# State space stage: both channel halves of a state in one VectorE product and scan and one GpSimd product of 1024 columns

## Chip, core and metric

The program runs on one core of a Trainium2 chip: TensorE (matmul), VectorE (DVE), ScalarE (ACT), GpSimd (POOL), and SyncE (SP), which issues the transfers. The metric is the time of one execution on the device in microseconds, here the median of three runs.

## What is computed

The reference is a network of two layers on 16 sequences of 256 positions with 128 features. Only the mamba block inside it is touched. It is, with 256 channels and 16 states a channel:

```python
h = layernorm(x, ln_g, ln_b)
xs, gate = jnp.split(h @ in_w, 2, axis=-1)
xs = jax.nn.silu(depthwise_conv(xs, conv_w) + conv_b)        # 4 taps
Bm, Cm = jnp.split(xs @ xp_w, 2, axis=-1)
dt = jax.nn.softplus(Bm @ dt_w + dt_b)
A = -jnp.exp(A_log)

def step(hst, inp):
    xt, dtt, Bt, Ct = inp
    dA = jnp.exp(dtt[..., None] * A)
    hst = hst * dA + dtt[..., None] * Bt[:, None, :] * xt[..., None]
    return hst, jnp.sum(hst * Ct[:, None, :], -1)
...
y = (y + D_skip * xs) * jax.nn.silu(gate)
return y @ out_w + res
```

## The kernel before

`state_space` (L1811) is one of fourteen stages that run one after the other. It goes through 8 turns (`TURNS`) of two sequences each. A tile has the 128 channels of one half (`CT` = 2 halves) on its partitions and the 512 positions of the two sequences (`T2`) as columns. For each of the 16 states (`N`) and each half, that is for 32 slots `w_` in a turn (`WS`), five engines pass one tile on:

- ScalarE, `decay` (L2074): dA = exp(A dt), 510 columns, into one of four places of dA. The first column of each sequence stays zero, which restarts the scan.
- TensorE, `spread_b` (L2223), once a state: the row of B spread over 128 partitions, into one of two PSUM banks BB, two states ahead.
- VectorE, `inflow` (L2122): the product of du = dt x and B, into one of two PSUM banks BU. It is issued one slot ahead, so the product of slot u+1 stands in front of the scan of slot u.
- VectorE, `scan` (L2132): the recurrence along the columns, into one of four places of hs.
- GpSimd, `weigh` (L1984): hs times the row of C, into one of four places of hc. SyncE fetches that row for all partitions, four states ahead (`Cs`).
- TensorE, `add_up` (L2230): hc through the identity, summed over the 16 states in the PSUM banks YS. It runs two slots behind.

Each of these waits for the engine that reads its place to be done with it. With four places, the scan of slot u waits for the product of slot u-4 on GpSimd, `weigh` for the sum of slot u-4, and `decay` for the scan of slot u-4.

All other work of a turn is written into the same loops by slot, in the tables `DVE_AT`, `POOL_AT`, `ACT_AT` and `PE_AT`. Most of it prepares the next turn: `stats` and `apply` (layer norm, VectorE; four `tensor_scalar` at L2119), `power` (GpSimd), `hn` and `h` (ScalarE), the transposes `h`, the convolution `x0` and `x1` (slots 10 and 11), `g0` and `g1`, `bc`, `dt0` and `dt1` (TensorE), `silu`, `bc`, `abs`, `exp`, `log` (ScalarE), and on GpSimd `split` (B in three bfloat16 parts), `dt` and `du`. The PSUM banks F0 and F1 are handed round among TensorE's pieces in the order of their issue. The rest, `gate`, `out` and `add`, finishes the turn before. An engine takes its queue in order, so a piece that waits holds every later slot on that engine. TensorE's queue at slot 10, for example, is `spread_b` of state 7, `add_up` of slot 8, `x0`.

## Time and profile before

| | |
|---|---|
| median of 3 runs | 4903.26 us (4899.63 to 4903.86) |
| profiled execution | 4894.49 us, its span 4892.8 us |
| VectorE busy over the span | 3405.3 us (70%) |
| TensorE / GpSimd / ScalarE busy | 3823.4 / 2392.6 / 2341.8 us |
| state space stage, first product to last sum | 545 us, 11% of the span |
| VectorE's product and scan in it | 256 of 695 ns and 256 of 1212 ns |
| GpSimd's product | 256 of 1271 ns |

The shares over the whole span are means over fourteen stages with different limits. For this change the stage has to be read alone: first the table of windows for it, then its groups of instructions, then the timeline of one of its turns.

### The profile page before, as it was taken

Reading aid. Unit: us, or ns where it says so; the run is one execution under the profiler, and the core shown is the slowest. Engines: PE = TensorE matmul, PEld = TensorE weight load, DVE = VectorE, ACT = ScalarE, POOL = GpSimd, SP = SyncE. Lnnn points to the kernel's source line nnn. Section 1 sums busy time; section 2 is a strip of 40 time slices with the busy share of each in tenths; the row PEclk is TensorE's granted clock in tenths of the full one; section 3 lists DMA queues with packets and bytes.
Section 4 is the critical chain, followed back from the end, with each engine's and each line's share of the span. In section 5 each row is a group of like instructions: output and inputs, shape, how many; then the busy total and the mean of one; then the engine's idle time right before and its main releaser. Section 6 shows DMA issues by size and latency. Waiting matters only on the chain. (4 is left out here: it accounts for less than half of the span.)

```text
span 4892.8 us, 90894 instructions
## 1 busy us (share of the span) xinstructions
PE 3823.4 (78%) x25840; PEld 2727.7 (56%) x25840; DVE 3405.3 (70%) x9524; ACT 2341.8 (48%) x5537; POOL 2392.6 (49%) x3948
## 2 busy tenths in 40 slices
PE   7889797779999799468868947568776887699475
PEld 5666565656666466366656636523332665466365
DVE  7888675556666677556658856669998664588566
ACT  3444464356666466234436634345553454266343
POOL 5666453434444443346644444367776663144443
PEclk9999898789999899689989968879988999899688
DMA  6000232100000133043323311211121331133113
GB/s 236 0 0 1 103 124 85 52 22 1 0 0 0 58 123 113 29 126 109 105 76 120 117 37 54 70 52 62 63 63 55 122 112 42 42 123 115 36 55 86
DMA packets 244547, 341.24 MB, mean 70 GB/s; under 512 B 26976, under 2 KB 187120, under 8 KB 243120
## 3 DMA queue, kind: packets, MB, share of 16 engines
q1 hardware_dynamic: 230960, 309.19, 19.0%
q0 software_dynamic: 13184, 27.22, 1.6%
q8 instruction: 186, 3.05, 0.3%
q14 instruction: 217, 1.78, 0.1%
HBM read 182.77 MB, written 147.26 MB: 67 GB/s over the span
## 5 line engine op out<-in xcount | busy, mean ns | idle before, releaser
L544 DVE TENSOR_REDUCE l0att_rowmax<-l0att_S 128x2 f32<-128x512 f32 x512 | 339.1, 686 | 130.6 <-PE l0att_S L724 128.5
L916 POOL TENSOR_TENSOR wb_prob<-wb_prob,wb_rden 128x128 f32<-128x128 f32 (+1 forms) x512 | 248.9, 508 | 360.7 <-DVE wb_rden L1093 360.2
L544 DVE TENSOR_REDUCE l1ffn_rowmax<-l1ffn_S 128x2 f32<-128x512 f32 x512 | 337.2, 686 | 90.9 <-PE l1ffn_S L724 83.5
L1990 POOL TENSOR_TENSOR ssm_hc<-core_AW_all,ssm_Cs 128x512 f32<-128x512 f32 x256 | 321.1, 1271 | 129.7 <-DVE core_AW_all L2136 96.6
L1455 POOL DMA_INDIRECT results<-e_y,e_back x220 | 210.6, 957 | 304.5 <-DVE e_y L1670 289.5
L958 ACT ACTIVATE wb_prob<-wb_biased,wb_nmax 128x128 f32<-128x128 f32 (+1 forms) x512 | 228.6, 447 | 236.9 <-DVE wb_nmax L1086 234.5
L2235 PE MATMUL ssm_Y<-ssm_hc,core_ident 128*128 128x512 f32 x512 | 288.6, 674 | 56.7 <-POOL ssm_hc L1990 30.5
L2136 DVE TENSOR_TENSOR_SCAN core_AW_all<-core_AW_all,ssm_U 128x512 f32<-128x512 f32 x256 | 310.3, 1212 | 1.1 <-ACT core_AW_all L2079 1.1
L724 PE MATMUL l1ffn_S<-l1ffn_K,l1ffn_Q 128*128 128x512 f32 x512 | 250.2, 492 | 76.9 <-DVE l1ffn_rowmax L544 44.7
L724 PE MATMUL l0att_S<-l0att_K,l0att_Q 128*128 128x512 f32 x512 | 246.8, 485 | 65.6 <-DMA l0att_K<-bounce 51.8
L2079 ACT ACTIVATE core_AW_all<-ssm_dt,ssm_A 128x510 f32<-128x510 f32 x256 | 178.5, 716 | 221.5 <-DVE core_AW_all L2136 219.8
L1782 PE MATMUL e_H<-e_xT,e_W1s 128*128 128x128 f32 x1760 | 249.3, 286 | 24.9 <-issue 20.4
L1086 DVE CUSTOM_DVE_ANT_0 wb_biased<-wb_S,wb_added 128x128 f32<-128x128 f32 (+1 forms) x512 | 162.8, 355 | 150.6 <-PE wb_S L1191 105.5
L1441 POOL DMA_INDIRECT routed<-e_rows,e_pos_i x192 | 187.0, 974 | 143.0 <-DVE e_pos_i L1601 93.6
L1782 PEld LDWEIGHTS e_H<-e_xT,e_W1s 128*128 128x128 f32 x1760 | 219.5, 196 | 54.4 <-issue 49.6
L1794 PE MATMUL e_Y<-core_W,e_hidden 128*128 x1760 | 233.6, 276 | 0.9 <-ACT e_hidden L1498 0.9
L1498 ACT ACTIVATE e_hidden<-e_H,e_b1s 128x128 f32<-128x128 f32 x568 | 162.4, 368 | 138.8 <-PE e_H L1782 116.4
L958 ACT ACTIVATE wa_prob<-wa_biased,wa_nmax 128x128 f32<-128x128 f32 (+1 forms) x256 | 114.3, 447 | 238.4 <-DVE wa_nmax L1086 238.4
L2129 DVE TENSOR_TENSOR ssm_U<-ssm_du,ssm_B 128x512 f32<-128x512 f32 x256 | 177.7, 695 | 56.5 <-POOL ssm_du L1981 37.5
L1794 PEld LDWEIGHTS e_Y<-core_W,e_hidden 128*128 128x128 f32 x1760 | 215.3, 193 | 1.5 <-issue 1.2
L737 PE MATMUL l0att_T<-l0att_Q,l0att_K 128*128 128x256 f32 x1024 | 209.1, 288 | 1.8 <-DMA l0att_Q<-l0att_maxT 1.5
L1191 PE MATMUL wb_S<-wb_kT,wb_qT 128*128 128x128 f32 (+1 forms) x1024 | 209.7, 328 | 0.0
(498 smaller groups left out, 11451.3 us busy)
## 6 DMA issues: line engine op xcount, KB each, us to landing
bounce<-l0att_parts SPq DMA_DIRECT2D x128, 256.0 KB, 2.8
bounce<-l1ffn_parts SPq DMA_DIRECT2D x128, 256.0 KB, 2.8
ssm_Cs<-c_rows SPq DMA_DIRECT2D x128, 256.0 KB, 3.0
routed<-core_Y SPq DMA_DIRECT2D x8, 2048.0 KB, 24.8
l0att_Q<-bounce SPq DMA_DIRECT2D x128, 128.0 KB
l0att_K<-bounce SPq DMA_DIRECT2D x128, 128.0 KB
bounce<-l1att_parts SPq DMA_DIRECT2D x64, 256.0 KB, 2.8
l1ffn_Q<-bounce SPq DMA_DIRECT2D x128, 128.0 KB
```

The source lines that it names most:

```text
L544: dve.tensor_reduce(out=rowmax[:, jp, qt, 2 * pair:2 * pair + 2], in_=S[a % 2][:].rearrange("p (j k) -> p j k", j=2)[:, :, 0:keys(qt)], op ...
L724: ins = pe.matmul(out[:, :, 0:keys(qt)], Q[:, n % 2, jp, pair, tile(qt)], K[:, n % 2, jp, :, pair, 0:keys(qt)], start=not causal, stop=Tru ...
L737: ins = pe.matmul(bank[:, j2 * L + q0:(j2 + 1) * L], K[:, n % 2, jp, j2, m, tile(kt)], Q[:, n % 2, jp, m, q0:L], start=True, stop=True)
L916: ins = pool.tensor_tensor(out=prob[:, w_ % NP, a:b], in0=prob[:, w_ % NP, a:b], in1=rden[:, w_ % NP, n:n + 1].to_broadcast([P, b - a]), o ...
L958: ins = act.activation(prob[:, w_ % NP, a:b], biased[:, w_ % 2, a:b], ACT.Exp, scale=-1.0, bias=nmax[:, w_ % NP, n:n + 1], accum_out=total ...
L1191: ins = pe.matmul(S[w_ % 2][:, a:b], qT[:, m % SLOTS, s * L + t * P:s * L + (t + 1) * P], kT[:, m % SLOTS, j, s * L:s * L + b - a], start= ...
L1455: pool.indirect_dma_start(core.results, bass.IndirectOffsetOnAxis(ap=back[:, j % RING, 1:2], axis=0), y[:, j % RING, :], None).then_inc(y_ ...
L1782: ins = pe.matmul(H[j % 2][:, f * P:(f + 1) * P], W1s[:, j % 2, f * P:(f + 1) * P], xT[:, j % 2], start=True, stop=True)
L1794: ins = pe.matmul(YB[j % 2][:, 0:D], hidden[:, j % 2, f], core.W2[:, bass.ds(e, 1), f, :].rearrange("p o d -> p (o d)"), start=f == 0, sto ...
L1990: pool.tensor_tensor(out=hc[:, u % 4], in0=hs[:, u % 4], in1=Cs[:, n % 4], op=ALU.mult)\
L2136: dve.tensor_tensor_scan(hs[:, u % 4], dA[:, u % 4], BU[u % 2][:], 0.0, ALU.mult, ALU.add)\
L2235: pe.matmul(YS[c][:], core.ident[:], hc[:, u % 4], start=n == 0, stop=n == N - 1)\
```

## The change

- `inflow`, `scan` and `weigh` run once per state on 1024 columns (both halves) instead of once per slot on 512. B and C are read by both halves through an axis of step zero.
- BU becomes one buffer of two PSUM banks. The product of a state is issued right in front of its scan and waits for the scan before; the scan waits for the product.
- dA, hs and hc hold two places of 1024 columns instead of four of 512. `scan` of state u now waits for `weigh` of state u-2, `weigh` for both sums of state u-2, and `decay` (still one instruction per half) for the scan of state u-2.
- `add_up`, `spread_b` and all of TensorE's and ScalarE's slots stay. The entries of `DVE_AT` and `POOL_AT` are given in states. On GpSimd each stands behind the same products as before. On VectorE `stats`, `gate` and `apply` come one half later, `add` stays.

```diff
@@ -1814,18 +1814,18 @@


     N, CT = 16, 2
-    WS = N * CT
+    HALVES = N * CT
     T2 = 2 * L
     with ExitStack() as ctx:
         sb, ps, sig = allocator(nc, ctx, name)
         F = [ps("F0"), ps("F1")]
         BB = [ps("B0"), ps("B1")]
-        BU = [ps("U0"), ps("U1")]
+        BU = ps("U", (P, CT * T2))
         YS = [ps("Y0"), ps("Y1")]


-        DVE_AT = {0: "stats", 2: "gate", 4: "apply", 7: "add"}
-        POOL_AT = {1: "power", 19: "split", 25: "dt", 27: "du"}
+        DVE_AT = {0: "stats", 1: "gate", 2: "apply", 3: "add"}
+        POOL_AT = {0: "power", 9: "split", 12: "dt", 13: "du"}
         ACT_AT = {9: "hn", 12: "h", 17: "silu", 20: "bc", 22: "abs0", 23: "abs1", 24: "exp", 25: "log"}
         PE_AT = {5: ("out",), 7: ("h",), 10: ("x0",), 11: ("x1",), 13: ("g0", "g1"), 15: ("bc",), 18: ("dt0", "dt1")}
         ROUNDS = range(-1, TURNS + 1)
@@ -1860,10 +1860,10 @@
         du = sb("du", [P, 2, CT, T2])
         A = sb("A", [P, CT, N])
         one = sb("one", [P, 1])
-        dA = core.AW_all[:, 0:4 * T2].rearrange("p (b t) -> p b t", b=4)
-        hs = core.AW_all[:, 4 * T2:8 * T2].rearrange("p (b t) -> p b t", b=4)
+        dA = core.AW_all[:, 0:4 * T2].rearrange("p (b c t) -> p b c t", b=2, c=CT)
+        hs = core.AW_all[:, 4 * T2:8 * T2].rearrange("p (b c t) -> p b c t", b=2, c=CT)
         Cs = sb("Cs", [P, 4, T2])
-        hc = sb("hc", [P, 4, T2])
+        hc = sb("hc", [P, 2, CT, T2])
         yg = sb("yg", [P, CT, T2])
         stats = sb("stats", [P, GT, 6])
         mv = sb("mv", [P, GT, 2])
@@ -1881,8 +1881,8 @@
         c_stored, c_sent = sig("c_stored", 16), [sig(f"c_sent{b}") for b in range(4)]
         split, magnitude, relued = sig("split"), sig("magnitude", CT), sig("relued", CT)
         dt_exp, log_made, dt_made, du_made = sig("dt_exp"), sig("log_made"), sig("dt_made"), sig("du_made", CT)
-        b_made, bu_made, dA_made = sig("b_made", N), sig("bu_made", WS), sig("dA_made", WS)
-        scanned, hc_made, summed = sig("scanned", WS), sig("hc_made", WS), sig("summed", WS)
+        b_made, bu_made, dA_made = sig("b_made", N), sig("bu_made", N), sig("dA_made", HALVES)
+        scanned, hc_made, summed = sig("scanned", N), sig("hc_made", N), sig("summed", HALVES)
         skipped, gated, added = sig("skipped", CT), sig("gated", CT), sig("added")
         dve_step, pool_step = sig("dve_step"), sig("pool_step")
         block = ctx.enter_context(nc.Block())
@@ -1923,7 +1923,7 @@
                     if inside(r):
                         g = r * N + n
                         sp.wait_ge(c_stored.sem, c_stored.at(r, 16))
-                        await_(sp, hc_made, CT * (g - 3))
+                        await_(sp, hc_made, g - 3)
                         sp.dma_start(Cs[:, g % 4, :], core.c_rows[r % 2, n:n + 1].to_broadcast([P, T2]))\
                             .then_inc(c_sent[g % 4].sem, 16)
                     if n == 12 and inside(r + 1):
@@ -1959,7 +1959,7 @@
             def split_b(j):
                 taken(pool, "bc", j)
                 await_(pool, b_made, b_made.at(j - 2, N))
-                await_(pool, hc_made, (j - 1) * WS + max(w for w in POOL_AT if POOL_AT[w] == "split") + 1 if j else 0)
+                await_(pool, hc_made, (j - 1) * N + max(n for n in POOL_AT if POOL_AT[n] == "split") + 1 if j else 0)
                 step(pool.tensor_copy(bc3[0:32, j % 2], bc[:]))
                 step(pool.tensor_tensor(out=left[:, 0], in0=bc[:], in1=bc3[0:32, j % 2], op=ALU.subtract))
                 step(pool.tensor_copy(bc3[32:64, j % 2], left[:, 0]))
@@ -1976,25 +1976,24 @@
             def times_x(j):
                 pool.wait_ge(dt_made.sem, j + 1)
                 pool.wait_ge(activated.sem, activated.at(j, CT))
-                await_(pool, bu_made, bu_made.at(j - 2, WS))
+                await_(pool, bu_made, bu_made.at(j - 2, N))
                 for c in range(CT):
                     pool.tensor_tensor(out=du[:, j % 2, c], in0=dt[:, j % 2, c], in1=xc[:, j % 2, c], op=ALU.mult)\
                         .then_inc(du_made.sem, 1)

-            def weigh(r, w_):
-                n, u = r * N + w_ // CT, r * WS + w_
+            def weigh(u):
                 pool.wait_ge(scanned.sem, u + 1)
-                if w_ % CT == 0:
-                    pool.wait_ge(c_sent[n % 4].sem, 16 * (n // 4 + 1))
-                await_(pool, summed, u - 3)
-                pool.tensor_tensor(out=hc[:, u % 4], in0=hs[:, u % 4], in1=Cs[:, n % 4], op=ALU.mult)\
+                pool.wait_ge(c_sent[u % 4].sem, 16 * (u // 4 + 1))
+                await_(pool, summed, CT * (u - 1))
+                pool.tensor_tensor(out=hc[:, u % 2], in0=hs[:, u % 2],
+                                   in1=Cs[:, u % 4, None, :].to_broadcast([P, CT, T2]), op=ALU.mult)\
                     .then_inc(hc_made.sem, 1)

             for r in ROUNDS:
-                for w_ in range(WS):
+                for n in range(N):
                     if inside(r):
-                        weigh(r, w_)
-                    if r == -1 and w_ == 2:
+                        weigh(r * N + n)
+                    if r == -1 and n == 1:
                         pool.wait_ge(again_ready.sem, 1)
                         for g in range(3):
                             rows = sel[32 * g:32 * g + 32]
@@ -2007,7 +2006,7 @@
                                            in1=core.in_w[:, None, 0:CT * P].to_broadcast([P, 4, CT * P]),
                                            op=ALU.mult).then_inc(selected.sem, 1)
                         pool.wait_ge(selected.sem, 4)
-                    x = POOL_AT.get(w_)
+                    x = POOL_AT.get(n)
                     if x and inside(r + 1):
                         {"power": power, "split": split_b, "dt": add_dt, "du": times_x}[x](r + 1)

@@ -2056,7 +2055,7 @@
                     c = int(x[3])
                     made(act, f"dt{c}", j)
                     await_(act, dt_made, j)
-                    await_(act, dA_made, dA_made.at(j - 2, WS))
+                    await_(act, dA_made, dA_made.at(j - 2, HALVES))
                     await_(act, du_made, du_made.at(j - 2, CT))
                     act.activation(ab[:, c, :], bank(f"dt{c}", j)[:], ACT.Abs, bias=core.dt_b[:, c:c + 1])\
                         .then_inc(magnitude.sem, 1)
@@ -2072,15 +2071,16 @@
                     act.activation(ab[:], lg[:], ACT.Ln, bias=one[:, 0:1]).then_inc(log_made.sem, 1)

             def decay(r, w_):
-                n, c, u = w_ // CT, w_ % CT, r * WS + w_
+                n, c, u = w_ // CT, w_ % CT, r * N + w_ // CT
                 if w_ == 0:
                     act.wait_ge(dt_made.sem, r + 1)
-                await_(act, scanned, u - 3)
-                act.activation(both(dA[:, u % 4])[:, :, 1:L], both(dt[:, r % 2, c])[:, :, 1:L], ACT.Exp,
+                if c == 0:
+                    await_(act, scanned, u - 1)
+                act.activation(both(dA[:, u % 2, c])[:, :, 1:L], both(dt[:, r % 2, c])[:, :, 1:L], ACT.Exp,
                                scale=A[:, c, n:n + 1]).then_inc(dA_made.sem, 1)

             for r in ROUNDS:
-                for w_ in range(WS):
+                for w_ in range(HALVES):
                     if inside(r):
                         if r == 0 and w_ == 0:
                             act.wait_ge(a_made.sem, 2)
@@ -2120,24 +2120,25 @@
                                       ALU.subtract, ALU.mult).then_inc(kept.sem, 1)

             def inflow(u):
-                r, n, c = u // WS, u // CT, u % CT
-                if u % WS == 0:
+                r, n = u // N, u % N
+                if n == 0:
                     dve.wait_ge(du_made.sem, du_made.at(r, CT))
-                if c == 0:
-                    dve.wait_ge(b_made.sem, n + 1)
-                await_(dve, scanned, u - 1)
-                dve.tensor_tensor(out=BU[u % 2][:], in0=du[:, r % 2, c], in1=BB[n % 2][:], op=ALU.mult)\
+                dve.wait_ge(b_made.sem, u + 1)
+                await_(dve, scanned, u)
+                dve.tensor_tensor(out=BU[:].rearrange("p (c t) -> p c t", c=CT), in0=du[:, r % 2],
+                                  in1=BB[u % 2][:, None, :].to_broadcast([P, CT, T2]), op=ALU.mult)\
                     .then_inc(bu_made.sem, 1)

             def scan(u):
+                dve.wait_ge(dA_made.sem, CT * (u + 1))
+                await_(dve, hc_made, u - 1)
                 dve.wait_ge(bu_made.sem, u + 1)
-                dve.wait_ge(dA_made.sem, u + 1)
-                await_(dve, hc_made, u - 3)
-                dve.tensor_tensor_scan(hs[:, u % 4], dA[:, u % 4], BU[u % 2][:], 0.0, ALU.mult, ALU.add)\
+                dve.tensor_tensor_scan(hs[:, u % 2].rearrange("p c t -> p (c t)"),
+                                       dA[:, u % 2].rearrange("p c t -> p (c t)"), BU[:], 0.0, ALU.mult, ALU.add)\
                     .then_inc(scanned.sem, 1)

             def gate(j):
-                dve.wait_ge(summed.sem, summed.at(j, WS))
+                dve.wait_ge(summed.sem, summed.at(j, HALVES))
                 dve.wait_ge(activated.sem, activated.at(j, 2 * CT))
                 for c in range(CT):
                     dve.scalar_tensor_tensor(out=YS[c][:], in0=xc[:, j % 2, c], scalar=core.d_skip[:, c:c + 1],
@@ -2156,19 +2157,15 @@
                                   op=ALU.add).then_inc(taken_sem("out", j), 1)

             for r in ROUNDS:
-                for w_ in range(WS):
+                for n in range(N):
                     if inside(r):
-                        u = r * WS + w_
-                        if u == 0:
-                            inflow(0)
-                        if u + 1 < TURNS * WS:
-                            inflow(u + 1)
-                        scan(u)
-                    x = DVE_AT.get(w_)
+                        inflow(r * N + n)
+                        scan(r * N + n)
+                    x = DVE_AT.get(n)
                     if x and inside(turn_with(x, r)):
                         {"stats": statistics, "gate": gate, "apply": apply, "add": add}[x](turn_with(x, r))
-                    if r == -1 and w_ == 5:
-                        dve.memset(dA.rearrange("p b (s q) -> p (b s) q", s=2)[:, :, 0:1], 0.0)\
+                    if r == -1 and n == 2:
+                        dve.memset(dA.rearrange("p b c (s q) -> p (b c s) q", s=2)[:, :, 0:1], 0.0)\
                             .then_inc(zeroed.sem, 1)
                         dve.wait_ge(a_made.sem, 1)
                         dve.tensor_scalar(A[:], A[:], -1.0, None, ALU.mult).then_inc(a_made.sem, 1)
@@ -2223,25 +2220,26 @@
             def spread_b(n):
                 if n % N == 0:
                     pe.wait_ge(split.sem, n // N + 1)
-                await_(pe, bu_made, CT * (n - 1))
+                await_(pe, bu_made, n - 1)
                 pe.matmul(BB[n % 2][:], sel[:, n % N, :], bc3[:, n // N % 2, :], start=True, stop=True)\
                     .then_inc(b_made.sem, 1)

             def add_up(u):
-                r, n, c = u // WS, u % WS // CT, u % CT
-                pe.wait_ge(hc_made.sem, u + 1)
+                r, n, c = u // HALVES, u % HALVES // CT, u % CT
+                if c == 0:
+                    pe.wait_ge(hc_made.sem, u // CT + 1)
                 if n == 0:
                     await_(pe, gated, gated.at(r - 1, CT))
-                pe.matmul(YS[c][:], core.ident[:], hc[:, u % 4], start=n == 0, stop=n == N - 1)\
+                pe.matmul(YS[c][:], core.ident[:], hc[:, u // CT % 2, c], start=n == 0, stop=n == N - 1)\
                     .then_inc(summed.sem, 1)

             for r in ROUNDS:
-                for w_ in range(WS):
+                for w_ in range(HALVES):
                     n = r * N + w_ // CT + 2
                     if w_ % CT == 0 and 0 <= n < TURNS * N:
                         spread_b(n)
-                    if 0 <= r * WS + w_ - 2 < TURNS * WS:
-                        add_up(r * WS + w_ - 2)
+                    if 0 <= r * HALVES + w_ - 2 < TURNS * HALVES:
+                        add_up(r * HALVES + w_ - 2)
                     for x in PE_AT.get(w_, ()):
                         if inside(turn_with(x, r)):
                             piece(x, turn_with(x, r))
```

## Rows read from the trace of the kernel before

**Rows 1.** Table of windows, whole stage: length, busy us (count) of PE, PEld, DVE, ACT, POOL, clock.
```profile
3221.40:3766.40 545.00, 416.31 (x990) 163.41 (x990) 517.99 (x643) 277.41 (x395) 401.68 (x348) 0.92 0.19 61
```

**Rows 2.** Groups by line and shape, VectorE and GpSimd. Columns: busy us, mean ns, idle before.
```profile
L2136 DVE TENSOR_TENSOR_SCAN core_AW_all<-core_AW_all,ssm_U 128x512 f32<-128x512 f32 x256 | 310.3, 1212 | 1.1 <-ACT core_AW_all L2079 1.1
...
L2129 DVE TENSOR_TENSOR ssm_U<-ssm_du,ssm_B 128x512 f32<-128x512 f32 x256 | 177.7, 695 | 56.5 <-POOL ssm_du L1981 37.5 <-PE ssm_B L2227 4.3
...
L1616 DVE TENSOR_TENSOR e_ended<-e_upto,core_dispatch 128x568 f32<-128x568 f32 x2 | 1.5, 744 | 0.0
...
L1616 DVE TENSOR_TENSOR e_ended<-e_upto,core_dispatch 128x312 f32<-128x312 f32 x2 | 1.0, 476 | 0.0
...
L1990 POOL TENSOR_TENSOR ssm_hc<-core_AW_all,ssm_Cs 128x512 f32<-128x512 f32 x256 | 321.1, 1271 | 129.7 <-DVE core_AW_all L2136 96.6 <-PE ssm_Y L2235 32.6
...
L1974 POOL TENSOR_TENSOR ssm_dt<-ssm_dt,ssm_ab 128x1024 f32<-128x1024 f32 x8 | 18.8, 2355 | 4.3 <-ACT ssm_ab L2072 4.3
...
L357 POOL TENSOR_TENSOR core_X<-core_X,core_rows 128x256 f32<-128x256 f32 x16 | 11.8, 737 | 0.0
```

**Rows 3.** Table of waits, turns 1 to 6. Columns: us in total, times, longest.
```profile
DVE ssm_U L2129 <- PE ssm_B L2227: 3.7, 6, 0.6
...
DVE core_AW_all L2136 <- ACT core_AW_all L2079: 0.9, 6, 0.2
```

**Rows 4.** Timeline of VectorE, one turn: start us, length us, instruction.
```profile
3489.59 1.21 DVE L2136 TENSOR_TENSOR_SCAN core_AW_all<-core_AW_all,ssm_U 128x512 f32<-128x512 f32 x1
...
3515.13 1.21 DVE L2136 TENSOR_TENSOR_SCAN core_AW_all<-core_AW_all,ssm_U 128x512 f32<-128x512 f32 x1
...
3516.37 0.70 DVE L2129 TENSOR_TENSOR ssm_U<-ssm_du,ssm_B 128x512 f32<-128x512 f32 x1
...
3516.98 1.21 DVE L2136 TENSOR_TENSOR_SCAN core_AW_all<-core_AW_all,ssm_U 128x512 f32<-128x512 f32 x1
...
3518.29 0.70 DVE L2129 TENSOR_TENSOR ssm_U<-ssm_du,ssm_B 128x512 f32<-128x512 f32 x1
...
3557.45 1.21 DVE L2136 TENSOR_TENSOR_SCAN core_AW_all<-core_AW_all,ssm_U 128x512 f32<-128x512 f32 x1
```

**Rows 5.** Timeline of VectorE and GpSimd, `tensor_scalar` beside GpSimd's products.
```profile
3225.06 0.17 DVE L2114 TENSOR_SCALAR ssm_ve<-ssm_mv 128x4 f32<-128x4 f32 x1
...
3488.82 6.17 POOL L1990 TENSOR_TENSOR ssm_hc<-core_AW_all,ssm_Cs 128x512 f32<-128x512 f32 x5
...
3493.86 1.15 DVE L2114 TENSOR_SCALAR ssm_ve<-ssm_mv 128x4 f32<-128x4 f32 x1
...
3504.57 2.04 DVE L2119 TENSOR_SCALAR core_Y<-core_X,ssm_mv,ssm_rstd 128x128 f32<-128x128 f32 x4
...
3504.73 1.28 POOL L1990 TENSOR_TENSOR ssm_hc<-core_AW_all,ssm_Cs 128x512 f32<-128x512 f32 x1 [0.58 <-DVE core_AW_all L2136]
```

**Rows 6.** Timeline of the same turn, from `x0` to the splitting of B.
```profile
3518.21 3.60 PE L2196 MATMUL ssm_F<-ssm_hpad,ssm_taps 128*128 128x512 f32 x8
...
3531.79 1.94 ACT L2079 ACTIVATE core_AW_all<-ssm_dt,ssm_A 128x510 f32<-128x510 f32 x3
...
3533.69 1.88 PE L2235 MATMUL ssm_Y<-ssm_hc,core_ident 128*128 128x512 f32 x4
...
3534.88 2.49 POOL L1990 TENSOR_TENSOR ssm_hc<-core_AW_all,ssm_Cs 128x512 f32<-128x512 f32 x2 [1.38 <-PE ssm_Y L2235]
...
3542.12 7.42 POOL L1990 TENSOR_TENSOR ssm_hc<-core_AW_all,ssm_Cs 128x512 f32<-128x512 f32 x6
```

**Rows 7.** Table of windows, two stretches of the turn, and TensorE's timeline.
```profile
3501.00:3505.00 4.00, 3.78 (x5) 1.56 (x6) 3.96 (x7) 1.03 (x2) 2.84 (x4) 0.50 0.00 0
...
3541.50:3546.00 4.50, 2.73 (x8) 0.80 (x6) 4.36 (x6) 4.45 (x6) 4.42 (x5) 1.00 0.04 15
...
3501.22 3.75 PE L2235 MATMUL ssm_Y<-ssm_hc,core_ident 128*128 128x512 f32 x4 [3.32 <-DVE ssm_yg L2149]
```

**Rows 8.** Timeline of VectorE, the end of the stage.
```profile
3759.39 1.41 DVE L2143 SCALAR_TENSOR_TENSOR ssm_Y<-ssm_xc,core_d_skip,ssm_Y 128x512 f32<-128x512 f32 x2 [2.67 <-PE ssm_Y L2235]
```

## Prediction

> **What bounds the kernel now.** I looked for the stage first, because the change touches nothing outside it. By the table of windows the state space stage takes 545 us, and VectorE is busy for 518.0 of them, 95% [rows 1]; GpSimd has 401.7, TensorE 416.3, ScalarE 277.4. So what VectorE does there is paid in full, unless something else holds it. The groups of instructions then give the prices [rows 2], and the table of waits says how much of VectorE's idle time in six full turns has a cause: 3.7 us for B and 0.9 us for dA [rows 3]. Last I read the timeline of one turn (3490.8 to 3558.7): its last scan starts 67.86 us after that of the turn before [rows 4]. In it one wait per turn of 0.6 us and one of 0.16 us are all that VectorE loses to others, but both show how near the queues are to it. I call W the length of GpSimd's product, T(n) the end of the scan of state n (in the kernel before, of its second half).
>
> **VectorE's own gain.** In the kernel before, a product starts 0.03 us after the scan it waits for, 0.10 us when it also waits for B; but the scan starts 0.09 us before the product ends, since that scan waits for an older product (3516.37 + 0.70 against 3516.98) [rows 4]. Two pairs take 1.85 + 1.92 = 3.77 us. Afterwards product and scan depend on each other both ways. The product of 1024 columns: two rows of 312 and 568 columns differ by 268 ns, 1.05 ns a column, so 0.695 + 512 x 1.05 ns = 1.23 us [rows 2]. The scan: a fixed part like the product's 0.16 us leaves 1.05 us for 512 columns, so 1.21 + 1.06 = 2.27 us; its bound above is twice 1.21, 2.42, and for the two-bank result, which no row shows, the product's is twice 0.695, 1.39. Gaps 0.04 and 0.10. Sum 3.64 us a state, 0.13 us less. Bounds for the new gap: -0.09 as now, 0.10 as with two waits. The Trainium skill (VectorE: DVE Perf Modes, section The DRAIN you can't avoid) says that the next operation waits for an empty pipeline anyhow and that a semaphore costs nothing extra. The overlap of 0.09 us in this case's rows speaks against the first half; by that rule the new wait would be free: 0.13 us less in 8 states of seven turns and 16 of the last, so the total 9 us lower.
>
> **The product on GpSimd.** A sum of 1024 columns takes 2.355 us, one of 512 takes 1.27, and an operand that is repeated over an outer axis adds nothing visible (256 columns: 0.737) [rows 2]. So W goes from 1.27 to 2.36 us (bounds 2.17, the slope alone, and 2.54, twice the old). GpSimd issues less in total, but four places wait for one whole product instead of the first half of it. I walk a turn through them, from the end of the last turn's scans.
>
> **Turn start to T(4).** Before: 3490.80 to 3516.34, 25.54 us [rows 4]. Five states save 0.65. Here VectorE's `tensor_scalar` instructions stand: the one of 4 columns takes 0.17 us in the first turn, when no product runs, but 1.15 us in the later one, from 3493.86 to 3495.01, where GpSimd's run of products ends (3494.99); and the four of `apply` take 2.04 us because a product starts at 3504.73, 0.16 us after them, and they go on when it ends at 3506.01 [rows 5]. The Trainium skill (SBUF — State Buffer, section Who interferes with whom) has this as one port pair that VectorE's fast modes and GpSimd lock for a whole instruction; these rows agree. `apply` now follows scan 2, whose product starts at the same distance and lasts 1.08 us longer: +1.08. The small one costs +0.10. Result: 25.54 - 0.65 + 1.18 = 26.07.
>
> **T(4) to x0.** At slot 10 TensorE must sum the first half of state 4 before the convolution `x0`. That half comes 0.08 + 2.36 us after T(4), and with 0.92 for its latency and its two matmuls `x0` starts at T(4) + 3.36. Before it started at 3518.21, 1.87 after T [rows 4, 6]. +1.49.
>
> **x0 to T(12).** From here TensorE works off a full queue at one matmul in 0.43 us up to about 3537. The order of its instructions stays, so what it finishes lies as far behind x0 as now. State 9's product waits for both halves of state 7 to be summed: their four matmuls end at 3533.69 + 1.88 = 3535.57, 17.36 after x0, and GpSimd follows after some 0.17 (3534.88 now, when only the first half was asked for) [rows 6]. Product 2.36; then the splitting of B stands between it and the next product, 3537.37 to 3542.12 = 4.75; then state 10's product 2.36. Scan 12 needs it, because hs has only two places. 17.53 + 2.36 + 4.75 + 2.36 + 0.05 + 2.27 = 29.32 us from x0 to T(12). VectorE alone would need 8 x 3.64 - 3.36 = 25.76, so 3.56 us of stall stand here. It appears in three parts: B of state 8 (about 0.5), the decay of state 9, whose two halves ScalarE ends at 3531.79 + 0.61 + 0.72 = 14.91 after x0 [rows 6], (about 1.9, since scan 9 would start 13.0 after x0), and the product of state 10 (the rest).
>
> **T(12) to T(15).** 3 x 3.64 = 10.92. The turn: 26.07 + 3.36 + 29.32 + 10.92 = 69.67, against 67.86: +1.81.
>
> **What is late next.** TensorE has nothing but one B product while GpSimd splits and multiplies: over 4 us idle. After 3.32 us idle behind the gate, four ready matmuls took 3.75 us instead of 1.88, at a granted clock of 0.50, the 1.2 GHz level [rows 6, 7]. I take the same here: the sums of state 10 end 1.57 us after state 12's product could start, and behind that stand dt, state 13, du and state 14 without slack (2.36 x 4 + 2.50). State 14's product then ends some 1.3 us after the next turn's first scan could start. The same slow group behind the gate holds state 2's product to 0.6 us after T(2), so that the last `tensor_scalar` waits 0.2 longer. +1.5; a turn costs +3.3.
>
> **Sum.** Seven turns prepare their successor: 7 x 3.3 = 23.1. The eighth has neither split nor `apply`: -16 x 0.13 = -2.1. The end: VectorE now waits 2.67 us after the last scan [rows 8], afterwards for 2.36 + four matmuls of 1.88, with latencies 4.4: +1.7. Total +22.7 us. The profiled execution took 4894.49 us (span 4892.8, 1.7 around it), so 4917.2 there; on the median of the runs, 4903.26, it is 4926. Steps at nothing: the C rows are still fetched four states ahead, in 3 us of 14; ScalarE's and SyncE's queues keep their order; the du product is needed at the first product of a turn, now one pair later. The cover of the last is 0.1 us now and about 1 us after, less where the clock is low.
>
> **Rivals.**
> - VectorE alone sets the pace (faster). If the chain behind x0 stayed covered and the port cost nothing, a turn would save 16 x 0.13 and the 0.78 of waits, less 0.2: -2.7, in all -19, so 4884. It decides from where x0 to T(12) falls under 25.8 us; the full TensorE queue and the 4.75 us split speak against it. 12%.
> - The chain is right, but the clock stays up and `apply` does not lengthen: 7 x (1.81 - 1.08) - 0.4 = +5, so 4908. For it: with 2.73 us of work in 4.5 us, behind the split, TensorE kept its 2.4 GHz now [rows 7]. 20%.
> - The forecast, with its own range 4914 to 4938. 50%.
> - The low clock reaches x0's run, or the two-bank product costs 1.39: each microsecond per turn is 7 us. With 2 to 3 of them 4940 to 4947. For it: TensorE waits longer before the gate than now. 18%.
>
> **Numbers.** Bounds: gap -9 or +4; W -5 or +5 (four places, seven turns); scan +11; two-bank product +11. Taken with the rivals the range is 4893 to 4946. A difference under 0.2% (10 us) can't be told from none in this kernel. Faster 0.12, same 0.20, slower 0.68.
>
> **What would show it.** The scan at 2.27, VectorE's product at 1.23, GpSimd's at 2.36; a gap of 0.04 between product and scan; `apply` at about 3.1 us for four; scans that wait for GpSimd's product behind the split (the present table has none) and for ScalarE at state 9; TensorE at 0.50 behind the split; a turn near 71 us. Wrong would be: a scan of 1024 columns with another slope, or TensorE's queue behind x0 shorter than now.

## The result and the profile after

The changed kernel takes 4924.18 us (median of 5 runs) against 4900.85 us of the kernel before in the runs taken with it: ratio 1.0051, 95% interval 1.0035 to 1.0067, so 23 us slower. The forecast was +22.7. One of the five runs took 13834.02 us at a mean granted clock of 0.56 (the other four 4921.63 to 4935.53 at 0.89 to 0.90), as one of e9's eight took 5099.56 at 0.78; the ratios leave both out, the medians don't.

Table of windows of the changed kernel, the whole state space stage and 5 us behind the split (length, busy us and count of PE, PEld, DVE, ACT, POOL, clock, DMA):

```profile
3222.40:3794.20 571.80, 426.23 (x990) 171.21 (x990) 510.53 (x387) 270.74 (x395) 381.72 (x220) 0.89 0.19 58
...
3561.00:3566.00 5.00, 3.67 (x5) 1.42 (x6) 3.90 (x3) 4.96 (x6) 3.58 (x2) 0.56 0.20 64
```

From the first product to the end of `add` the stage takes 3222.46 to 3794.16 = 571.7 us; before it was 3221.43 to 3766.32 = 544.9. That is +26.8, and the 28.5 of the span leave 1.7 elsewhere. (The medians say +23.3. The profiled execution of the changed kernel, 4923.11, is near its median; that of the kernel before, 4894.49, lies 6.4 us under its own.) VectorE is busy for 7.5 us less than before [rows 1] and the stage is longer.

Groups of the changed kernel in the stage (busy us, mean ns, idle before):

```profile
L2136 DVE TENSOR_TENSOR_SCAN core_AW_all<-core_AW_all,ssm_U 128x1024 f32<-128x1024 f32 x128 | 292.7, 2287 | 37.4 <-ACT core_AW_all L2079 12.7 <-POOL ssm_hc L1988 9.8 <-DVE ssm_U L2128 0.5
...
L2128 DVE TENSOR_TENSOR ssm_U<-ssm_du,ssm_B 128x1024 f32<-128x1024 f32 x128 | 157.1, 1227 | 53.2 <-POOL ssm_du L1981 37.7 <-PE ssm_B L2224 5.7
...
L2119 DVE TENSOR_SCALAR core_Y<-core_X,ssm_mv,ssm_rstd 128x128 f32<-128x128 f32 x28 | 22.1, 851 | 0.0
...
L1988 POOL TENSOR_TENSOR ssm_hc<-core_AW_all,ssm_Cs 128x1024 f32<-128x1024 f32 x128 | 300.7, 2354 | 176.6 <-PE ssm_Y L2233 94.0 <-DVE core_AW_all L2136 81.6
```

The three prices asked for: scan 2.287 us (taken 2.27), product 1.227 (1.23), GpSimd's product 2.354 (2.36), against [rows 2]. Four `tensor_scalar` of `apply` cost 3.4 us by their mean of 851 ns, 3.24 as a block in the turn below, 2.04 before [rows 5].

Waits of six full turns, the second to the seventh (us in total, times, longest):

```profile
POOL ssm_hc L1988 <- PE ssm_Y L2233: 82.2, 38, 4.1
...
DVE core_AW_all L2136 <- ACT core_AW_all L2079: 10.9, 6, 1.8
...
DVE core_AW_all L2136 <- POOL ssm_hc L1988: 8.9, 10, 1.0
...
DVE ssm_U L2128 <- PE ssm_B L2224: 5.4, 6, 2.0
```

Against [rows 3] two old waits grew from 3.7 and 0.9 to 5.4 and 10.9 us, and one is new: VectorE behind GpSimd, six times in front of scan 12 and four times in front of a turn's first scan (turns 3, 4, 6 and 7).

One turn of the changed kernel, the fifth, in the timeline (start us, length us), and the first scan of the sixth:

```profile
3506.67 2.29 DVE L2136 TENSOR_TENSOR_SCAN core_AW_all<-core_AW_all,ssm_U 128x1024 f32<-128x1024 f32 x1
...
3510.17 1.24 DVE L2114 TENSOR_SCALAR ssm_ve<-ssm_mv 128x4 f32<-128x4 f32 x1
...
3520.93 3.24 DVE L2119 TENSOR_SCALAR core_Y<-core_X,ssm_mv,ssm_rstd 128x128 f32<-128x128 f32 x4
...
3529.58 2.29 DVE L2136 TENSOR_TENSOR_SCAN core_AW_all<-core_AW_all,ssm_U 128x1024 f32<-128x1024 f32 x1
...
3531.97 1.23 DVE L2128 TENSOR_TENSOR ssm_U<-ssm_du,ssm_B 128x1024 f32<-128x1024 f32 x1
...
3533.34 2.29 DVE L2136 TENSOR_TENSOR_SCAN core_AW_all<-core_AW_all,ssm_U 128x1024 f32<-128x1024 f32 x1
...
3535.32 3.60 PE L2193 MATMUL ssm_F<-ssm_hpad,ssm_taps 128*128 128x512 f32 x8
...
3559.93 4.65 POOL L1988 TENSOR_TENSOR ssm_hc<-core_AW_all,ssm_Cs 128x1024 f32<-128x1024 f32 x2
...
3562.33 3.78 PE L2233 MATMUL ssm_Y<-ssm_hc,core_ident 128*128 128x512 f32 x4 [3.46 <-POOL ssm_hc L1988]
...
3562.36 2.29 DVE L2136 TENSOR_TENSOR_SCAN core_AW_all<-core_AW_all,ssm_U 128x1024 f32<-128x1024 f32 x1 [0.98 <-POOL ssm_hc L1988]
...
3573.19 2.50 POOL L1981 TENSOR_TENSOR ssm_du<-ssm_dt,ssm_xc 128x512 f32<-128x512 f32 x2
...
3575.64 4.67 POOL L1988 TENSOR_TENSOR ssm_hc<-core_AW_all,ssm_Cs 128x1024 f32<-128x1024 f32 x2
...
3578.09 2.29 DVE L2136 TENSOR_TENSOR_SCAN core_AW_all<-core_AW_all,ssm_U 128x1024 f32<-128x1024 f32 x1 [0.82 <-POOL ssm_hc L1988]
```

The turn is 3578.09 - 3506.67 = 71.42 us long, 67.86 before [rows 4]. From first scan to first scan the seven turns take 67.87, 71.40, 72.34, 71.26, 71.42, 72.34 and 71.26 us, 497.9 together, 25.5 more than before; in the kernel before they are alike from the second on (67.86 to 67.89). A product starts at 3531.97 and the scan 1.37 later, 0.13 after the product's end; the next product follows the scan by 0.10. GpSimd starts state 10's product at 3559.93, behind the split; scan 12 waits for its end at 3562.3. TensorE's next four matmuls take 3.78 us, in a window at clock 0.56. The products of states 14 and 15 run from 3575.64, straight behind du, and the first scan of the next turn waits 0.82 us.

One thing in which the turns differ is the `tensor_scalar` of 4 columns. It takes 1.24 us in the second and fifth turn, 2.25 in the sixth, where a product of GpSimd has just started, and 0.17 in the seventh, where that product starts after it:

```profile
3581.48 2.34 POOL L1988 TENSOR_TENSOR ssm_hc<-core_AW_all,ssm_Cs 128x1024 f32<-128x1024 f32 x1 [1.17 <-PE ssm_Y L2233]
...
3581.60 2.25 DVE L2114 TENSOR_SCALAR ssm_ve<-ssm_mv 128x4 f32<-128x4 f32 x1
...
3653.93 0.17 DVE L2114 TENSOR_SCALAR ssm_ve<-ssm_mv 128x4 f32<-128x4 f32 x1
...
3654.20 2.35 POOL L1988 TENSOR_TENSOR ssm_hc<-core_AW_all,ssm_Cs 128x1024 f32<-128x1024 f32 x1 [1.54 <-PE ssm_Y L2233]
```

The last turn and the end of the stage, timeline of VectorE:

```profile
3738.70 0.69 DVE L2156 TENSOR_TENSOR core_Y<-ssm_F,core_Y 128x512 f32<-128x512 f32 x1 [1.16 <-PE ssm_F L2216]
...
3788.73 1.41 DVE L2144 SCALAR_TENSOR_TENSOR ssm_Y<-ssm_xc,core_d_skip,ssm_Y 128x512 f32<-128x512 f32 x2 [4.50 <-PE ssm_Y L2233]
...
3793.47 0.69 DVE L2156 TENSOR_TENSOR core_Y<-ssm_F,core_Y 128x512 f32<-128x512 f32 x1 [2.14 <-PE ssm_F L2216]
```

The wait behind the last scan is 4.50 us, 2.67 before [rows 8]. The wait behind it, for `out`, is 2.14; in the kernel before it is 3.64:

```profile
3765.63 0.69 DVE L2155 TENSOR_TENSOR core_Y<-ssm_F,core_Y 128x512 f32<-128x512 f32 x1 [3.64 <-PE ssm_F L2219]
```

### The profile page after: what moved, and what is told of

The parts are those of the page before. It is cut to its first block and busy times, and to the rows that moved or that the text cites. A ratio compares the mean times of both kernels' runs of the same rounds, so it can differ in the third digit from the quotient of the medians.

```text
span 4921.3 us, 90249 instructions
## 1 busy us (share of the span) xinstructions
PE 3834.1 (78%) x25840; PEld 2736.7 (56%) x25840; DVE 3398.1 (69%) x9268; ACT 2333.0 (47%) x5537; POOL 2367.7 (48%) x3820
## 5 line engine op out<-in xcount | busy, mean ns | idle before, releaser
L1988 POOL TENSOR_TENSOR ssm_hc<-core_AW_all,ssm_Cs 128x1024 f32<-128x1024 f32 x128 | 300.7, 2354 | 176.6 <-PE ssm_Y L2233 94.0
L2136 DVE TENSOR_TENSOR_SCAN core_AW_all<-core_AW_all,ssm_U 128x1024 f32<-128x1024 f32 x128 | 292.7, 2287 | 37.4 <-ACT core_AW_all L2079 12.7
L2233 PEld LDWEIGHTS ssm_Y<-ssm_hc,core_ident 128*128 128x128 f32 x512 | 105.4, 217 | 238.8 <-POOL ssm_hc L1988 128.6
L521 ACT ACTIVATE core_AW_all<-l1ffn_T 128x512 f32<-128x512 f32 x256 | 147.1, 598 | 132.8 <-PE l1ffn_T L737 132.0
```

The source lines that it names most:

```text
L1988: pool.tensor_tensor(out=hc[:, u % 2], in0=hs[:, u % 2], in1=Cs[:, u % 4, None, :].to_broadcast([P, CT, T2]), op=ALU.mult)\
L2136: dve.tensor_tensor_scan(hs[:, u % 2].rearrange("p c t -> p (c t)"), dA[:, u % 2].rearrange("p c t -> p (c t)"), BU[:], 0.0, ALU.mult, ALU ...
L2233: pe.matmul(YS[c][:], core.ident[:], hc[:, u // CT % 2, c], start=n == 0, stop=n == N - 1)\
```

## The experiments

"Stage" is the time from the first product to the end of `add` in each kernel's profile; it is 544.9 us in the kernel before and 571.7 in the changed one. Each is taken from one execution; in e10, whose time is that of the kernel before, it is 545.3. "Ratio" is against the kernel before in the same job, with its 95% interval.

| | stage us | median us | ratio |
|---|---|---|---|
| e1 halves on GpSimd | 552.1 | 4899.29 | 1.0018 (1.0008 to 1.0028) |
| e2 before + product of 1024 | 566.1 | 4914.76 | 1.0048 (1.0031 to 1.0064) |
| e3 apply behind gate | 572.2 | 4915.30 | 1.0046 (1.0029 to 1.0062) |
| e4 early waits | 568.6 | 4922.37 | 1.0068 (1.0051 to 1.0084) |
| e5 repeats of B | 565.4 | 4916.64 | 1.0036 (1.0022 to 1.0050) |
| e6 e3 + e5 | 555.5 | 4912.01 | 1.0023 (1.0012 to 1.0033) |
| e7 e1 + e3 + e4 + e5 | 543.9 | 4900.02 | 1.0002 (0.9992 to 1.0011) |
| e8 split one state later | 571.8 | 4926.71 (one run) | |
| e9 x0 one slot earlier | 564.3 | 4914.89 | 1.0037 (1.0025 to 1.0048) |
| e10 before, x0 earlier | 545.3 | 4901.81 | 1.0002 (0.9993 to 1.0012) |
| e11 e3 + e4 + repeats + e9 | 548.4 | 4908.43 | 1.0018 (1.0007 to 1.0029) |
| e12 e11 + e1 | 533.8 | 4889.91 | 0.9981 (0.9972 to 0.9991) |

**e1, GpSimd's product in halves.**

```diff
-                await_(pool, summed, CT * (u - 1))
-                pool.tensor_tensor(out=hc[:, u % 2], in0=hs[:, u % 2], in1=Cs[:, u % 4, None, :]...)
+                for c in range(CT):
+                    w_ = CT * u + c
+                    await_(pool, summed, w_ - 3)
+                    pool.tensor_tensor(out=hc[:, w_ % 4], in0=hs[:, u % 2, c], in1=Cs[:, u % 4], op=ALU.mult)...
```

> The changed kernel, but GpSimd multiplies by C in halves of 512 columns again (hc in four places of 512); VectorE's product and scan stay at 1024. Theory (the long GpSimd product is what costs): the transfer of state 4's first half to TensorE is 1.1 us earlier, the scale-and-shift instructions of the layer norm wait 1.1 us less, the block behind the split shrinks, so a turn goes from 71.4 to about 68 us and the total falls by some 20 us, to about 4903. Rival (VectorE's mutual waits between product and scan cost): the turn stays above 70 us and the total above 4915.

A turn is 68.54 us and the stage 19.6 us shorter. The merged product was most of the loss, but not in all of the places that the expectation names. x0 starts 2.48 us after T(4) instead of 3.45, and the `tensor_scalar` of 4 columns takes 0.17 us instead of 1.24. The four of `apply` still take 3.01 us, and the 29.40 us from x0 to T(12) are those of the changed kernel (29.33), so the block behind the split did not shrink.

```profile
3504.75 3.01 DVE L2120 TENSOR_SCALAR core_Y<-core_X,ssm_mv,ssm_rstd 128x128 f32<-128x128 f32 x4
```

**e2, the complement: only GpSimd's product merged, in the kernel before.**

```diff
+                pool.wait_ge(scanned.sem, CT * (n + 1))
+                await_(pool, summed, CT * (n - 1))
+                pool.tensor_tensor(out=hc[:, n % 2], in0=hs...[:, n % 2], in1=Cs[:, n % 4, None, :]...)
```

> The kernel before, but with only GpSimd's product merged to 1024 columns; VectorE keeps its products and scans of 512, one product ahead, and two BU banks. Theory (the long GpSimd product costs): TensorE's convolution starts 1.5 us later and the scan behind the split waits, 2 to 3 us per turn, so 4915 to 4923. Rival (VectorE's merge costs): within 5 us of the kernel before.

The stage grows by 21.2 us with VectorE's instructions untouched; turns of 69.2 to 71.5 us. Its waits from 3289 to 3690 us, nearly six turns:

```profile
DVE ssm_U L2128 <- PE ssm_B L2226: 19.9, 6, 3.9
...
DVE core_AW_all L2135 <- POOL ssm_hc L1988: 6.9, 5, 1.4
```

The first was 3.7 us before. So GpSimd's merged product costs some 20 us in either direction, and VectorE's own merge the remaining 6 to 7. Part of the 20 is TensorE's clock: in four turns of e2 the convolution x0 takes 4.65 to 5.30 us instead of 3.60. Both runs change the length of the product and the places of hc (two of 1024 or four of 512) together; which of the two costs more is not shown.

**e3, `apply` behind `gate`.**

```diff
-        DVE_AT = {0: "stats", 1: "gate", 2: "apply", 3: "add"}
+        DVE_AT = {0: ("stats",), 1: ("gate", "apply"), 3: ("add",)}
```

> The changed kernel, with apply moved from behind the scan of state 2 to directly behind gate, where GpSimd has finished state 1's product and waits for scan 2. Theory (the port that VectorE's fast instructions share with GpSimd): the four instructions take about 1.1 us instead of 3.24, a turn is 2.1 us shorter, in all -15 us, about 4909. Rival (the stall belongs to the instruction itself, or VectorE's time in this place is covered by a later wait): no change, 4924.

No gain in the stage; the expectation failed. The timeline shows two reasons (second turn, then the fifth):

```profile
3293.64 2.36 POOL L1988 TENSOR_TENSOR ssm_hc<-core_AW_all,ssm_Cs 128x1024 f32<-128x1024 f32 x1 [0.53 <-DVE core_AW_all L2136]
...
3295.97 1.11 DVE L2119 TENSOR_SCALAR core_Y<-core_X,ssm_mv,ssm_rstd 128x128 f32<-128x128 f32 x4
...
3509.51 2.35 POOL L1988 TENSOR_TENSOR ssm_hc<-core_AW_all,ssm_Cs 128x1024 f32<-128x1024 f32 x1
...
3510.05 2.66 DVE L2119 TENSOR_SCALAR core_Y<-core_X,ssm_mv,ssm_rstd 128x128 f32<-128x128 f32 x4
...
3527.60 5.29 PE L2193 MATMUL ssm_F<-ssm_hpad,ssm_taps 128*128 128x512 f32 x8
```

In the second turn GpSimd's product had ended at 3296.00 and the four took 1.11 us; in the five later turns the product started late (3509.51), and they took 2.61 to 2.66. What that still saved up to state 4 (1.5 us in the fifth turn, 1.2 on the mean of turns 2 to 7) went to a convolution at 5.29 us instead of 3.60: TensorE was at 1.2 GHz there in all of the turns 2 to 7.

**e4, waits in front of the product.**

```diff
+            EARLY = (1, 2, 3, 4, 5, 6, 7, 10)
+            def inputs(u):
+                dve.wait_ge(dA_made.sem, CT * (u + 1))
+                await_(dve, hc_made, u - 1)
...
             def inflow(u):
                 r, n = u // N, u % N
+                if n in EARLY:
+                    inputs(u)
...
             def scan(u):
-                dve.wait_ge(dA_made.sem, CT * (u + 1))
-                await_(dve, hc_made, u - 1)
+                if u % N not in EARLY:
+                    inputs(u)
```

> The changed kernel; for states 1 to 7 and 10 the waits for dA and for GpSimd stand in front of the product instead of between product and scan, so that only the wait for the product itself is left there. Theory A (the number of waits in front of an instruction sets the gap): the gap of 0.13 us between product and scan falls to about 0.04 in these eight states and stays in the others, while the gap from scan to product grows a little; at most 0.09 x 5 states x 7 turns + 0.09 x 8, -4 us. Theory B (a result in PSUM is seen late by the next instruction): all 16 gaps stay at 0.13 and the total at 4924.

One early state and one that is not:

```profile
3523.35 1.23 DVE L2136 TENSOR_TENSOR ssm_U<-ssm_du,ssm_B 128x1024 f32<-128x1024 f32 x1
...
3524.61 2.29 DVE L2144 TENSOR_TENSOR_SCAN core_AW_all<-core_AW_all,ssm_U 128x1024 f32<-128x1024 f32 x1
...
3559.86 1.23 DVE L2136 TENSOR_TENSOR ssm_U<-ssm_du,ssm_B 128x1024 f32<-128x1024 f32 x1
...
3561.22 2.29 DVE L2144 TENSOR_TENSOR_SCAN core_AW_all<-core_AW_all,ssm_U 128x1024 f32<-128x1024 f32 x1
```

3523.35 + 1.23 to 3524.61 is a gap of 0.03 us; 3559.86 + 1.23 to 3561.22 one of 0.13. Theory A holds for this gap in all eight states. The gap from scan to product, now with four waits in front, grows from 0.10 to 0.13, so a state gains 0.07 us. That the stage is 3.1 us shorter does not show this gain by itself: x0 takes 4.62 to 5.30 us in four turns here and 5.0 in two of the changed kernel. (The ratio is not better; 3 us is inside its interval.)

**e5, TensorE kept busy.**

```diff
+                for _ in range({3: 12, 5: 3, 6: 3, 7: 3, 13: 14}.get(n % N, 0)):
+                    pe.matmul(BB[n % 2][:], sel[:, n % N, :], bc3[:, n // N % 2, :], start=True, stop=True)
                 pe.matmul(BB[n % 2][:], ...).then_inc(b_made.sem, 1)
```

> The changed kernel, in which TensorE repeats its own B product into the same bank (same values) where it stands idle: 12 times in front of the wait for gate, 3 times each before the sums of states 3 to 5, 14 times while GpSimd splits B. Theory (TensorE's granted clock falls while it waits for GpSimd and the sums behind it are late): the groups of four sums take 1.9 us instead of 3.5 to 3.8, no convolution takes 5 us, the wait of 0.82 us of a turn's first scan goes, and a turn falls from 71.4 to 72.3 us to about 70.3, in all -8 to -14 us. Rival (the waits are GpSimd's own length, the clock is by the way): the turn stays at 71.3 or more.

TensorE behind the split, third turn:

```profile
3406.17 3.19 PE L2225 MATMUL ssm_B<-ssm_bc,ssm_sel 96*128 96x512 bf16 x14
...
3410.04 1.98 PE L2235 MATMUL ssm_Y<-ssm_hc,core_ident 128*128 128x512 f32 x4 [0.47 <-POOL ssm_hc L1988]
```

The four matmuls take 1.98 us instead of 3.78. Every convolution takes 3.60, the first scan of a turn no longer waits, and turns fall to 70.7 to 71.2; the stage by 6.3, less than the 8 to 14 expected. (In the ratios e5 and the changed kernel can't be told apart: 1.0022 to 1.0050 against 1.0035 to 1.0067.) **e6, with `apply` moved as well:**

> As e5, and apply behind gate as in e3_apply_behind_gate. In e3 the state 4 scan came 1.5 us earlier and a convolution at the 1.2 GHz level (5.29 us instead of 3.60) took it back. Theory (port and clock are two costs, one hid the other): a turn of about 69 us, -10 us against e5's stage or more than 1 us a turn. Rival (what apply gives is taken back by another wait whatever the clock): as e5.

68.8 to 69.2 us a turn, 9.8 us less than e5. Together the two give 16.2 us, alone -0.5 and 6.3: the clock had hidden what the port gave.

**e7, the four together.**

> VectorE's product and scan at 1024 columns, GpSimd's product in halves, apply behind gate, the repeats of e5, and the early waits of e4. Each of the four takes away one cost that the theory names: 68.5 us a turn with the halves alone, less some 1 for apply and the port, 0.5 for the gaps, so 66.5 to 67.5, below the 67.9 of the kernel before, in all -3 to -10 us against it. Rival (TensorE's full queue behind the convolution decides alone): 68.5 as in e1_pool_halves, so +7 us.

67.69 us a turn, the time of the kernel before, a little short of the expectation. Here x0 starts 3.15 us after T(4), 2.48 in e1: the repeats in front of state 4's sum now hold it back.

**e8, the split one state later** (`POOL_AT`: 9 becomes 10).

> The changed kernel, with the splitting of B one state later on GpSimd (behind state 10's product). Theory (scan 12 waits because the split of 4.75 us stands in front of state 10's product): its wait of about 1 us goes, and so does up to 1 us a turn, -3 to -7 us for the stage, unless dt, du and state 14's product are then late for the next turn. Rival (scan 12 would wait for ScalarE or TensorE in any case): the wait changes its cause and the turn stays.

Scan 12 no longer waits for GpSimd: in its second turn it starts 26.2 us after x0, 27.1 in the same turn of the changed kernel. But a later scan of each turn waits 1.3 us for GpSimd instead, and the first scan of the next one 0.5; the turns are 71.3 and 72.1 to 72.2 us, and the stage is as long as before the move. The expectation failed: in these two places the split costs the same.

**e9, the convolution one slot earlier, and e10, the same in the kernel before.**

```diff
-        ACT_AT = {9: "hn", 12: "h", ...
-        PE_AT = {5: ("out",), 7: ("h",), 10: ("x0",), 11: ("x1",), 13: ("g0", "g1"), 15: ("bc",), 18: ("dt0", "dt1")}
+        ACT_AT = {9: "hn", 11: "h", ...
+        PE_AT = {5: ("out",), 7: ("h",), 9: ("x0",), 10: ("x1",), 12: ("g0", "g1"), 14: ("bc",), 17: ("dt0", "dt1")}
```

> The changed kernel; TensorE's pieces x0, x1, g0 and g1, bc, dt0 and dt1 one slot earlier (half a state) and ScalarE's h at slot 11 instead of 12, so that x0 waits for state 3's product instead of state 4's. Theory (all three waits of VectorE between states 8 and 12 are TensorE's full queue, and that queue starts with x0): x0 starts 3 us or more earlier against the scan of state 4, g0 then waits for ScalarE for 1 to 2 us, and the stretch from scan 4 to scan 12 falls from 32.8 us to 30.5 to 31, so 2 us a turn and -14 us for the stage. Rival (the length of GpSimd's product and the split set it from state 9 on): less than 0.7 us a turn.

> The same move in the kernel before, as the control: there only 0.78 us a turn are lost to TensorE and ScalarE, so at most -5 us. If it gave as much as in e9, the move would be good for a reason of its own.

x0 starts 2.4 to 3.3 us earlier against T(4) and VectorE's waits for B and dA are gone. But the stretch from scan 4 to scan 12 only falls from 32.8 to 32.1 us, and in three of seven turns not at all; in these three x0 ran at a lower clock (4.39 to 4.65 us). Waits of e9 from 3289 to 3690 us, and TensorE in its fourth turn:

```profile
POOL ssm_hc L1988 <- PE ssm_Y L2233: 77.9, 35, 4.8
...
DVE core_AW_all L2136 <- POOL ssm_hc L1988: 17.3, 18, 2.0
...
3468.61 1.02 PE L2233 MATMUL ssm_Y<-ssm_hc,core_ident 128*128 128x512 f32 x2
...
3470.39 1.98 PE L2198 MATMUL ssm_F<-ssm_hpad,core_in_w 128*128 128x512 f32 x4 [0.76 <-ACTq L2041]
...
3472.21 1.02 PE L2233 MATMUL ssm_Y<-ssm_hc,core_ident 128*128 128x512 f32 x2
```

VectorE's wait for GpSimd took their place (8.9 us in the changed kernel). GpSimd itself waits for TensorE about as long as there (82.2 us in its six turns). Its product waits for both sums of an earlier state, and the rows of TensorE show a piece, g, between the two sums of one state; x1 and bc stand so too. In the changed kernel x0 and dt do. What this order costs is not shown. The rival was nearer. The stage still gained 7.4 us, in good part because the two turns of 34.5 us from scan 4 to scan 12 (those with x0 at 5.0 us) are gone. In the kernel before the move is worth nothing.

**e11 and e12, all of it, without and with the halves** (the repeats only in front of gate and behind the split).

> The changed kernel with GpSimd's product still at 1024 columns, and apply behind gate, early waits, the repeats of B in front of gate and behind the split, and the move of e9. 69.0 us a turn in e6, less 0.4 for the gaps and 2 for the queue: 66.5 to 67, so -5 to -9 us against the kernel before. If the long product is what costs in itself, it stays above 68.

> As e11, with GpSimd's product in halves as well. VectorE alone would need 16 x 3.70 + 6.2 = 65.4 us a turn; 65.5 to 66.5, so -10 to -17 us against the kernel before.

e11 takes 67.6 to 68.2 us a turn, more than the 66.5 to 67 expected, and is 0.18% slower than the kernel before instead of faster. e12 takes 66.15, as expected; its 9 us against the kernel before fall just short of the 10 to 17. First scans of two successive turns of e12:

```profile
3419.10 2.29 DVE L2145 TENSOR_TENSOR_SCAN core_AW_all<-core_AW_all,ssm_U 128x1024 f32<-128x1024 f32 x1
...
3485.25 2.29 DVE L2145 TENSOR_TENSOR_SCAN core_AW_all<-core_AW_all,ssm_U 128x1024 f32<-128x1024 f32 x1
```

Both differ only in GpSimd's product, and the stage by 14.6 us: the long product costs also where everything else has been made room for. e12 is faster than the kernel before, by 0.19% (0.09 to 0.28%), and so than the changed one. That the merge on VectorE is what gains is not shown: of the other edits only the move of x0 was also tried in the kernel before, not the repeats or the place of `apply`.

## Why the prediction was right, and where it was off

The turn, step by step, for the turn shown above and on the mean of turns 2 to 7:

| step | predicted us | fifth turn us | mean us |
|---|---|---|---|
| last scan to T(4) | 26.07 | 26.69 | 27.06 |
| T(4) to x0 | 3.36 | 3.45 | 3.54 |
| x0 to T(12) | 29.32 | 29.33 | 29.82 |
| T(12) to T(15) | 10.92 | 11.26 | 11.26 |
| wait of the first scan | 1.3 | none | 0.82 in four of seven |

The last row is inside the first one where it occurs, and 0.13 us of it is the ordinary gap. With the 1.5 us for what is late next, the forecast of a turn was 71.17 us; the mean is 71.67.

- **VectorE's own gain** was mis-sized: 0.13 us a state predicted, 0.02 measured (3.77 to 3.75). The term is the new gap, 0.04 against 0.13 us. I took the gap of one wait; three waits stand there. By e4 it is 0.03 with one. Both steps that VectorE alone sets are longer by this (5 and 3 states). The Trainium skill (VectorE: DVE Perf Modes, "The DRAIN you can't avoid") has it that a semaphore costs nothing beyond the pipe's emptying; no run here bears that out for several, since the gap was 0.03 us with one wait in front, 0.10 with two and 0.13 with three.
- **GpSimd's product** was right in size (2.354 us, 2.36 taken), and e1 and e2 show from both sides that it is the cause of most of the loss. e1 shows one place that doesn't hold: with products of 512 columns x0 to T(12) stays at 29.40 us.
- **The port.** `apply` takes 3.12 to 3.25 us (3.1 predicted). Shown by e3, where it takes 1.11 us if no product runs. The `tensor_scalar` of 4 columns was to cost 0.10 more in every turn; it costs 1.24 us in three turns, 2.25 to 2.27 in two and 0.17 in two, against about 1.15 before. The first step takes 26.2 to 28.3 us; the turn shown lies below the mean.
- **The queue behind x0** came out to 0.03 us in the five turns with x0 at 3.60 us, with its three waits: 0.34 for B, 1.81 for dA, 0.98 for GpSimd. e9 shows that the first two really are TensorE's queue, but also that scan 12 then waits longer for GpSimd, so that little is won.
- **The clock** behind the split fell as predicted (four matmuls 3.78 us, 3.75 taken); the wait it causes was 0.82 instead of 1.3, and stands in front of turns 3, 4, 6 and 7 only. e5 and e6 show the clock as its cause. With the ordinary gap taken off the wait is 2.8 us in all, where 7 x 1.3 = 9.1 were forecast: this term was 6.3 us too large. The error in VectorE's gain goes the other way, by 0.11 us in 72 states (8 in each of seven turns and 16 in the last), 7.9 us, so the two nearly cancel. What I gave to a rival, a convolution at 1.2 GHz, happened too, in two of the seven turns (5.0 us); there the two steps from T(4) to T(12) take 1.7 us more.
- **The end.** Last turn and end together were to give -0.4 us and took +1.2 (71.28 to 72.46 from that turn's first scan). From its first scan to the end of its last the last turn takes 0.86 us more, not 2.1 less: 1.8 are the missing gain per state, and 1.16 a wait that the forecast doesn't have, that of `add` for `out`. The wait behind the last scan grew by 1.83 (1.7 predicted), but the next one, for `out`, shrank by 1.5 (3.64 to 2.14): `out` ran at a granted clock of 1.00 from 3790 to 3793.5 us, in the kernel before at 0.61 from 3761 to 3764.5. No run explains why, and in e1, e5 and e6 that wait is 3.55 to 3.76 again.

So the seven turns cost +25.5 for 23.1 and the end +1.2 for -0.4. The stage grew by 26.8 us and the two profiled executions differ by 28.5; that the sum of +22.7 agrees with the medians' 23.3 is partly luck.

Not settled: why TensorE's clock is low at x0 in some turns of the changed kernel and high in others. With it the time of one and the same stage moves by some us, so differences of 3 us between the stages of two experiments are not told by their edits alone.

## What to carry to other kernels

Merging two instructions saves a fixed part once, but everyone who waited for the first half now waits for the whole: look for the consumers of the first half, and for the queue that each of them heads. A buffer of two large places is not one of four small ones: whoever fills it waits for the whole place. And a neighbour's longer instruction can lock out one's own: price it where both overlap, and expect turns that were alike to differ, because the overlap shifts.

## What the runs showed of the hardware

- With one wait in front, a VectorE instruction starts 0.03 us after the one that it depends on, with two 0.10, with three 0.13, though the other waits had long been met; with four (e4) it is 0.13 too. Where none of three waits was for the instruction just in front, in the kernel before, it started 0.09 us before that one's end.
- VectorE's `tensor_scalar` stands still while a GpSimd product runs: 1.11 us for four, or 2.66 and 3.24. One of 4 columns takes 0.17 us if it starts before the product and 2.25 if it starts 0.12 us after it.
- Repeating a matmul that nobody needs made the stage shorter, by 6.3 us (e5 against the changed kernel), though it can't be told from none in the ratios: behind an idle stretch of 3.5 us the granted clock was at its lower level (0.56 over 5 us) and four matmuls took 3.78 us; with the stretch filled they took 1.98.
